# Gathering routed rows in 256-byte pieces, with one block transpose for sixteen, and the router's logits one step earlier

## What is computed

```python
x = x + tanh(g_xattn) * attention(layernorm(x), ctx)      # causal self attention plus cross attention
h = layernorm(x)
out = expert(h, sg, su, sd)                                # shared expert, hidden size 704
probs = softmax(h @ wr.T + rb)                             # 7 routed experts
scores, idx = top_k(probs, 2); scores /= scores.sum()
for e in range(7):
    out += w[..., e] * expert(h, rg[e], ru[e], rd[e])      # w: the two scores, else 0
x = x + tanh(g_ffn) * out
# expert(h, g, u, d) = (silu(h @ g.T) * (h @ u.T)) @ d.T
```

## Time and profile before

| | us |
|---|---|
| median of three runs | 1286.07 |
| lowest and highest run | 1285.67 and 1287.56 |
| time of the profiled execution | 1287.56 |
| its span | 1285.8 |
| PE busy in the span | 1259.2 (98%) |
| DVE, ACT, POOL busy | 1022.2, 851.3, 388.0 |
| granted TensorE clock, mean | 0.994 of full |

### The profile page before, as it was taken

One profiled execution on the slowest core, in us unless ns is written; L12 is line 12 of the kernel. 1 busy time (PEld: TensorE's weight loads), 2 busy tenths in 40 slices (PEclk: granted clock), 3 DMA queues, 4 the chain that ended last, 5 costly groups with the idle time before them and its releaser, 6 DMA issues.

```text
span 1285.8 us, 24163 instructions
## 1 busy us (share of the span) xinstructions
PE 1259.2 (98%) x7868; PEld 689.2 (54%) x7869; DVE 1022.2 (79%) x2357; ACT 851.3 (66%) x1243; POOL 388.0 (30%) x628
## 2 busy tenths in 40 slices
PE   8989999999999999999999999999999999999997
PEld 5645333333333333333333333254568999999996
DVE  6788899999999999999999999554534777777673
ACT  4654788888888888888888888743212555455552
POOL 6565211242242242332422412430001333333332
PEclk9999899999999999999999999999999999999999
DMA  8784332332433523423324334336915122222221
GB/s 250 231 247 144 99 85 85 106 117 79 122 98 85 147 87 99 126 83 107 109 82 129 103 79 141 107 106 166 252 37 148 34 36 35 35 33 37 37 33 21
DMA packets 91864, 133.58 MB, mean 104 GB/s; under 512 B 21387, under 2 KB 56331, under 8 KB 91642
## 3 DMA queue, kind: packets, MB, share of 16 engines
q1 hardware_dynamic: 83162, 122.16, 33.2%
q0 software_dynamic: 7296, 9.97, 4.9%
q10 hardware_dynamic: 1312, 0.27, 0.1%
HBM read 84.36 MB, written 47.55 MB: 103 GB/s over the span
## 4 chain that ended last, share of the span: by engine, by line
PE 90%; DVE 1%; issue 1%; DMA 1%; ACT 1%; POOL 0%; POOLq 0%; SPq 0%; DVEq 0%
PE ps L835 18%; PE ps L989 15%; PE ps L815 14%; PE ps L711 13%; PE ps L1018 8%; PE ps L948 6%; PE ps L963 3%; PE ps L818 3%; PE ps L723 2%; PE ps L789 2%; PE ps L719 2%; PE ps L715 1%; PE ps L923 1%; DMA arena<-rowst 1%; PE ps L803 1%
## 5 line engine op out<-in xcount | busy, mean ns | idle before, releaser
L1510 DVE TENSOR_REDUCE mx<-ps 128x1 f32<-128x512 f32 (+3 forms) x960 | 594.3, 653 | 46.1 <-PE ps L711 19.2
L1180 ACT ACTIVATE arena<-ps 128x1024 f32<-128x1024 f32 (+1 forms) x512 | 480.4, 989 | 67.4 <-PE ps L815 59.8
L835 PE MATMUL ps<-arena 128*32 128x512 f32 (+3 forms) x2048 | 273.0, 567 | 0.8 <-issue 0.4
L1399 POOL TENSOR_SCALAR_AFFINE_SELECT arena<-arena 128x128 f32<-128x128 f32 x256 | 75.3, 294 | 492.2 <-ACT arena L1180 486.0
L815 PE MATMUL ps<-arena 98*128 98x512 bf16 x624 | 198.6, 381 | 1.8 <-DMA arena<-rowst 1.7
L711 PE MATMUL ps<-arena 96*128 96x512 bf16 x576 | 197.6, 382 | 1.9 <-DMA arena<-k_parts 1.4
L989 PEld LDWEIGHTS ps<-work,arena 128*128 128x128 f32 x1672 | 192.7, 192 | 2.9 <-issue 0.9
L989 PE MATMUL ps<-work,arena 128*128 128x128 f32 x1672 | 193.1, 275 | 0.8 <-issue 0.8
L1827 DVE STREAM_TRANSPOSE work<-wp 32x64 f32<-32x64 f32 x608 | 143.3, 236 | 8.5
L835 PEld LDWEIGHTS ps<-arena 128*32 128x32 f32 x2048 | 54.1, 108 | 103.6 <-issue 86.7
L711 PEld LDWEIGHTS ps<-arena 96*128 96x128 bf16 x576 | 53.9, 97 | 96.3 <-DVE mx L1510 55.6
(11 more groups left out here) (191 smaller groups left out, 1527.4 us busy)
## 6 DMA issues: line engine op xcount, KB each, us to landing
o_parts<-work SPq DMA_DIRECT2D x63, 256.0 KB, 2.9
arena<-in_experts SPq DMA_DIRECT2D x56, 176.0 KB
arena<-k_parts SPq DMA_DIRECT2D x48, 198.1 KB, 3.1
arena<-k_parts SPq DMA_DIRECT2D x48, 132.1 KB, 2.9
arena<-in_experts SPq DMA_DIRECT2D x7, 768.0 KB
k_parts<-work SPq DMA_DIRECT2D x16, 300.0 KB, 3.8
q_parts<-work SPq DMA_DIRECT2D x12, 384.0 KB, 3.2
arena<-q_parts SPq DMA_DIRECT2D x48, 96.0 KB, 2.2
```

What stands on the lines that cost most here:

```text
L835: mm = pe.matmul(ps[32 * q:32 * q + VW, 6, first:T], vst[:, r % VR, TT + kt if cross else kt, :], pr[:, c0:c0 + T - first], start=(phase = ...
L1180: act.activation(pr[:, c0:c0 + n], ps[:, 2 * (g % 2):2 * (g % 2) + 2, :].rearrange("p b n -> p (b n)")[:, 0:n], ACT.Exp, scale=SCALE).then ...
L1399: pool.affine_select(out=exps, in_=exps, pattern=[[1, P]], compare_op=ALU.is_ge, fill=0.0, base=0, channel_multiplier=-1).then_inc(S["mask ...
L1510: return dve.tensor_reduce(m, out, AX_X, ALU.max)
```

## The change

Four parts.

1. **Gather in pieces.** `xn_rows` is read as rows of 64 floats (256 bytes), four to a token. `gather(i)` becomes four indirect DMAs, one for each quarter q of `xg`'s columns; lane p of quarter q takes piece p // 32 of the token of lane 32 q + p % 32. With the rows laid out so, `rows_turned` is one DVE transpose of 128x256 in place of sixteen.
2. **Picking.** The row numbers must be laid out to match. POOL builds `pick` (a copy of the identity's blocks) in `wp` and fills `piece_no` with four memsets, behind `logits_turned`. PE's new `pick_lanes()`, four matmuls of 128x128 by 38 columns, stands in the middle of `shared_down(2)`, and DVE's new `piece_rows()` turns them into piece numbers. `rows_ready2` is gone with the cast; `pieces_ready` takes its place before gather(0) and `shared_down(3)`.
3. **Logits earlier.** `logits()` moves ahead of `shared_up(1, 1, 2)`, on PE and ACT, and `turn_logits()` ahead of `shared_up(1, 2, 3)`. DVE's `shared_hidden(1, 1, 2)` and `(1, 2, 3)` each go behind one more piece of the routing.
4. **Banks and DVE's order.** `XN_BANK` no longer uses the bank of the logits, and DVE scales the rows of sequence 2 (`scaled(2)`) two hidden steps earlier.

```diff
-XN_BANK = [0, 1, 4, 5, 6, 7, 4, 5]
+XN_BANK = [0, 1, 4, 5, 6, 4, 5, 6]
...
+        pick = wp[:, :, :].rearrange("p k (q t) -> p (k q) t", q=2)
-        row_at = bv[:, 2, NSLOT:2 * NSLOT].bitcast(U32)
+        piece_row = bv[:, 2, NSLOT:NSLOT + 4 * NSLOT].bitcast(U32).rearrange("p (q i) -> p q i", q=4)
+        piece_no = bv[:, 2, C - 1:C]
+        xn_pieces = xn_rows.rearrange("n (j w) -> (n j) w", w=PIECE)
...
-                    pe.wait_ge(S["rows_ready2"], 1)
+                    pe.wait_ge(S["pieces_ready"], 1)
...
+            def pick_lanes():
+                pe.wait_ge(S["pick_ready"], 5)
+                pe.wait_ge(S["routed"], 1)
+                for q in range(4):
+                    mm = pe.matmul(ps[:, 6, q * NSLOT:(q + 1) * NSLOT], pick[:, q, :], back, start=True, stop=True)
+                mm.then_inc(S["picked"], 1)
...
             turn_xn(3)
+            logits()
             shared_up(1, 1, 2)
-            logits()
-            shared_up(1, 2, 3)
             turn_logits()
-            shared_up(1, 3, IT)
+            shared_up(1, 2, IT)
...
-            shared_down(2)
+            shared_down(2, 0, TT // 2)
+            pick_lanes()
+            shared_down(2, TT // 2, TT)
             shared_down(3)
...
             xn_out(3)
-            shared_silu(1, 1, 2)
             act.wait_ge(S["logits_mm"], 1)
             act.activation(logit_rows, ps7[:, :], ACT.Copy).then_inc(S["logits_out"], 1)
-            shared_silu(1, 2, IT)
+            shared_silu(1, 1, IT)
...
+            pool.wait_ge(S["logits_turned"], 1)
             pool.wait_ge(S["rest_zeros"], 3)
+            pool.tensor_copy(pick.rearrange("p q (j c) -> p q j c", j=4),
+                             ident[:, :].rearrange("p (q c) -> p q c", q=4).unsqueeze(2).to_broadcast([P, 4, 4, QUARTER])
+                             ).then_inc(S["pick_ready"], 1)
+            for j in range(4):
+                pool.wait_ge(S["pick_ready"], j + 1)
+                pool.memset(piece_no[j * QUARTER:(j + 1) * QUARTER, :], float(j)).then_inc(S["pick_ready"], 1)
...
-                pool.indirect_dma_start(out=xg[:, i % 2, :], out_offset=None, in_=xn_rows,
-                                        in_offset=bass.IndirectOffsetOnAxis(row_at[:, i:i + 1], 0)
-                                        ).then_inc(gathered[i % 2], 16)
+                for q in range(4):
+                    pool.indirect_dma_start(out=xg[:, i % 2, q * PIECE:(q + 1) * PIECE], out_offset=None, in_=xn_pieces,
+                                            in_offset=bass.IndirectOffsetOnAxis(piece_row[:, q, i:i + 1], 0)
+                                            ).then_inc(gathered[i % 2], 16)
...
-            shared_hidden(0, 1, 4)
+            shared_hidden(0, 1, 2)
             dve.wait_ge(S["num_in"], 16 * NQ * (NGRP + 2))
             dve.wait_ge(S["den_in"], 16 * NQ * (NGRP + 2))
             scaled(2)
-            shared_hidden(0, 4, 5)
+            shared_hidden(0, 2, 5)
...
+            def piece_rows():
+                dve.wait_ge(S["picked"], 1)
+                dve.tensor_scalar(piece_row.rearrange("p q i -> p (q i)"), ps[:, 6, 0:4 * NSLOT], 4.0, piece_no, ALU.mult, ALU.add
+                                  ).then_inc(S["pieces_ready"], 1)
...
-                for j in range(4):
-                    for r in range(4):
-                        ins = dve.transpose(xgT[j * QUARTER:(j + 1) * QUARTER, b, :, r * QUARTER:(r + 1) * QUARTER],
-                                            xg[r * QUARTER:(r + 1) * QUARTER, b, j * PIECE:(j + 1) * PIECE].rearrange(
-                                                "r (h c) -> r h c", h=2))
+                dve.transpose(xgT[:, b, :, :].rearrange("p h (q r) -> p q h r", q=4),
+                              xg[:, b, :].rearrange("p (q h c) -> p q h c", q=4, h=2)).then_inc(S["xT_ready"], 1)
```

More of the change, by code:

```diff
@@ L355, in program @@
                  "shared_load routed_load route_load up_mm silu_done h_done rest_zeros down_mm acc_done gathered0 gathered1 xT_ready "
-                 "copied up2_mm silu2_done h2_done down2_mm y_ready scattered based routed rows_ready2").split()
+                 "copied up2_mm silu2_done h2_done down2_mm y_ready scattered based routed pick_ready picked pieces_ready").split()
         S = {n: sem(n) for n in names}
@@ L934, in turn_xn @@
                         pe.wait_ge(S["xn_freed"], 1 + XN_BANK.index(XN_BANK[2 * b + k]))
-                    layer_turn(xn_bank(2 * b + k), b, k).then_inc(S["xn_turned"], 1)
+                    layer_turn(ps[:, XN_BANK[2 * b + k], :], b, k).then_inc(S["xn_turned"], 1)
             def shared_up(tb, it0=0, it1=IT):
@@ L1207, in xn_out @@
                     act.wait_ge(S["xn_turned"], n + 1)
-                    act.activation(xnT[:, b, n % 2, :], xn_bank(n), ACT.Copy).then_inc(S["xn_freed"], 1)
+                    act.activation(xnT[:, b, n % 2, :], ps[:, XN_BANK[n], :], ACT.Copy).then_inc(S["xn_freed"], 1)
             def shared_silu(tb, it0=0, it1=IT):
@@ L1460, in _ @@
             pool.wait_ge(S["rows_out"], 32)
-            pool.wait_ge(S["rows_ready2"], 1)
+            pool.wait_ge(S["pieces_ready"], 1)
             gather(0)
@@ L1699, in _ @@
             scaled(3)
-            shared_hidden(1, 0, 2)
+            shared_hidden(1, 0, 1)
             link(dve.memset(lg[:, :, NE:E8], -3e38))
@@ L1719, in _ @@
             first_largest(lg, m1, s1)
-            shared_hidden(1, 2, 3)
+            shared_hidden(1, 1, 2)
             link(dve.scalar_tensor_tensor(out=lg[:, :, :], in0=s1[:, :, :], scalar=-3e38, in1=lg[:, :, :],
@@ L1815, in finish_table @@
                 link(dve.tensor_scalar(back, result_at, float(NTOK), -float(NTOK), ALU.is_ge, ALU.mult))
[L1816 to L1819, removed]
-            def rows_turned(i, b):
-                dve.wait_ge(gathered[b], (i - b) * 8 + 16)
-                for j in range(4):
-                    for r in range(4):
-                        ins = dve.transpose(xgT[j * QUARTER:(j + 1) * QUARTER, b, :, r * QUARTER:(r + 1) * QUARTER],
-                                            xg[r * QUARTER:(r + 1) * QUARTER, b, j * PIECE:(j + 1) * PIECE].rearrange(
-                                                "r (h c) -> r h c", h=2))
-                ins.then_inc(S["xT_ready"], 1)
+                dve.tensor_tensor(back, result_at, back, ALU.add).then_inc(S["routed"], 1)
+            def piece_rows():
+                dve.wait_ge(S["picked"], 1)
+                dve.tensor_scalar(piece_row.rearrange("p q i -> p (q i)"), ps[:, 6, 0:4 * NSLOT], 4.0, piece_no, ALU.mult, ALU.add
+                                  ).then_inc(S["pieces_ready"], 1)
+            def rows_turned(i, b):
+                dve.wait_ge(gathered[b], (i - b) * 32 + 64)
+                dve.transpose(xgT[:, b, :, :].rearrange("p h (q r) -> p q h r", q=4),
+                              xg[:, b, :].rearrange("p (q h c) -> p q h c", q=4, h=2)).then_inc(S["xT_ready"], 1)
             def hidden(i, b):
@@ L1860, in turn @@
                 result(i - 1, 1 - b, first)
-            shared_hidden(1, 3, IT)
+            shared_hidden(1, 2, IT)
             token_weights()
@@ L1875, in _ @@
             finish_table()
+            piece_rows()
             shared_out(2)
```

2 lines of the change are left out of this document (removed).

## The result

The kernel after takes 1328.41 us (median of 4 runs, 1326.69 to 1330.72) where the kernel before took 1285.87 in the same comparison: a ratio of 1.0334, 95% interval 1.0315 to 1.0354. It is 42.5 us slower; the forecast was 2.3, and its range ended at 1291.8. The profiled execution has a span of 1325.2 us, 39.4 more than before, at a mean granted clock of 0.996.

What follows compares the result with a forecast made beforehand. The prediction took PE as the bound, with no idle time in the routed stage. Terms 2.45 - 0.10 + 0.95 - 1.01 = +2.29 us on 1286.07 gave 1288.4 us (+0.18%), range 1285.6 to 1291.8.

Steps and rivals of the forecast that it cites:

- POOL in the loop: Routed loop: four gathers, a scatter and gaps take POOL 7.04 or 7.6 us a turn against PE's 7.50; small excess harmless.
- POOL becomes the bound: Rival, routed loop: gathers costing 1.58 us make POOL's turn 9.4, about 1343 us in all; 0.13 together with serial DMAs.
- if the turn is longer than 7.50: Sign, routed loop: a turn above 7.50 us would show the forecast wrong.
- scaled(2), "nothing": DVE's scaling moved beside POOL's work: 2.38 us, product ready at 867.0 before PE needs it at 867.95, so no cost.
- Logits: logits() straight behind turn_xn(3): PE waits 2.22 us for ACT's copies plus 0.23 restart, +2.45 us.
- bank term: turn_xn(2), second half in bank 4: the following step needs no restart, -0.10 us, between -0.2 and +0.3.
- Pick: Four matmuls of 128x128 by 38 columns on PE's path in shared_down(2): +0.95 us, bounds 0.48 and 1.73.
- Transpose: DVE's one 128x256 transpose replacing sixteen (3.97 us together): taken as 0.5 us, off the chain in the loop.
- The gap before slot 1: Start of routed stage: PE's 0.77 us wait before slot 1 and a 0.24 restart go, -1.01 us.
- The first slots come late: Rival, start of routed stage: slot 0's pieces land late, PE waits up to 3 us, 1289.5 to 1291.5; chance 0.07.
- The wait at the logits isn't there: Rival: ACT or the banks behave otherwise, so without the 2.45 us the time is 1285.9; chance 0.06.
- Faster: Rival, loop: DVE's sixteen transposes slowed PE's reading by 0.15 us a turn; removing them gives 1283.0 us; chance 0.04.

Runs made afterwards that it cites:

- four losing versions: The kernel after with a 32x1 memset behind each slot's second gather, behind its fourth, behind both, or already-met waits between gathers: 1328.74, 1332.46, 1330.43, 1327.51 us.
- Four pieces without scatters: The kernel before with its gather cut into four of 256 bytes a row and the scatter left out for all slots but the last: 1304.11 us.
- the kernel that has nothing else: The kernel before with only the new places of the logits, the bank list and DVE's order: 1288.48 us, ratio 1.0024.
- the kernel after with memsets: The kernel after with a memset of 32x1 on POOL behind each gather: 1289.78 us, ratio 1.0031.
- the two versions without the loss in the loop: The kernel after with a 32x1 memset behind each gather, 1289.78 us, or with a slot's gathers in two pairs, the second behind `h2_done`, 1289.84 us.
- two pieces: The kernel before with its one gather a slot cut into two of 512 bytes a row: 1282.62 us, ratio 0.9982.
- the pairs without scatters: The kernel before with four 256-byte gathers a slot in two pairs, the second behind `h2_done`, and no scatters but the last: 1282.84 us.
- three pieces: The kernel before with its one gather a slot cut into three of 512, 256 and 256 bytes a row: 1282.86 us, ratio 0.9986.

## Why the prediction was wrong

**The step that failed** is "POOL in the loop". Its number was right: a turn of POOL came out at 7.04 to 7.6 us, and the trace has 6.98 from one scatter to the next when POOL doesn't wait (1046.45 to 1053.43). The gather that I took at 0.99 has a median of 952 ns. What failed is the inference from it: that a POOL which keeps up costs nothing. I asked only whether POOL would become the bound, and for the rival "POOL becomes the bound" only what a dearer gather would do. The gather wasn't dearer, POOL had idle time, and the turn still went from 7.50 to 8.6 us. The condition that I wrote, "if the turn is longer than 7.50", came true by another way. The runs show this much of the cause: time is lost with four gathers a turn, with the scatter or without it, and not with three or two; most of it comes without small pieces, and it comes in full without the change's transposes and routing; POOL's busy time alone costs nothing. While POOL issues its groups of DMAs, ACT and DVE take up PE's finished work 3 to 6.5 us late, and they go on 1.2 to 1.35 us after a group of ten has ended. With three gathers ACT is up to 1.6 us late already, and the turn still takes 7.50.

**What stays open** is what holds the others up, and what decides whether it happens. Four memsets of 0.12 us or a step tied to `h2_done` in each turn remove the whole loss; one or two memsets, or waits, remove none; and the same row of twelve gathers was harmful in one kernel and harmless in another. Neither the pace nor the number in a row explains these. A rival is left that no run tests by itself, the pauses. Between 1010 and 1240 the kernel after and its four losing versions go in groups of ten DMAs with no pause over 0.32 us inside, and the versions that lose nothing pause for 0.5 us or more after five DMAs at most. Four pieces without scatters lose with groups of four, though, and whether a pause prevents the lateness or is there because DVE's results come in time, no run tells. No run shows the mechanism, and I name none.

**scaled(2), "nothing"**, was the second miss. I bounded it by the 2.38 us of the earlier trace rows. In the kernel after the four operations stand beside POOL's tensor_tensors at 860.59, 861.82 and 863.27 and take 5.24 us; in other kernels with this order 3.83, 4.08, 4.24 and 4.58. Alone they take 1.38. The prediction left 0.95 us to spare (867.95 less 867.0); 5.24 is 2.86 more than the 2.38 it counted with, and PE waited 1.8:

```profile
PE ps L894 <- ACT xnT L1215: 2.2, 1, 2.2
PE ps L946 <- DVE arena L1651: 1.8, 1, 1.8
PE ps L699 <- ACT xnT L1215: 1.4, 1, 1.4
```

The row taken as a bound was one case of partial overlap, not the worst. The Trainium skill has a rule for it ("SBUF — State Buffer", section "Who interferes with whom"): a tensor_scalar can take a port pair that VectorE shares with GpSimd, and then one of the two waits until the other's instruction is through. The trace agrees with it: three of POOL's operations of about 1.3 us lie in the 5.24, and their 3.85 us and DVE's 1.38 alone make 5.23.

**The terms that held.** Logits: +2.45 was forecast, with a wait of 2.2; the wait is the first row above, and with the bank term of -0.10 (a wait of 1.4 instead of 1.5) the forecast of +2.35 stands against +2.31 in the kernel that has nothing else. Pick: 0.82 us against 0.95. Transpose: 435 ns against 0.5. The gap before slot 1: in the kernel after with memsets the chain has one piece of 9.82 us for slots 0 and 1, twice 4.91, and no gap, so the -1.01 is there once the stops are gone. By these, 2.31 + 0.82 - 1.01 and 2.15 for scaled(2) (the 5.28 us that the stretch grew in the kernel after, less 2.31 and 0.82) make 4.27; the two versions without the loss in the loop are 4.5 us over before. So without the failed step the answer would have been 2 us low.

**The rivals.** "The first slots come late" did not occur as such: no wait of PE for a slot is seen. "The wait at the logits isn't there" was wrong by its row above. "POOL becomes the bound" was priced at 1343 and lies nearer the measured time than the forecast, but not for its reason: a gather took 952 ns and not 1.15 us or more, and POOL had idle time. "Faster": the last kernels show no turn under 7.50, so DVE's sixteen transposes did not slow PE. The rule of the Trainium skill that I cited against the small transfers ("DMA: Bandwidth & Descriptors") speaks of their fixed cost; two and three pieces cost nothing in the loop, and four gathers with a memset behind each cost nothing either, so that cost wasn't the reason, though its advice to join them would have avoided the loss.

## What to carry to other kernels

An engine that keeps up with the loop can still slow it: before a turn is given more indirect DMAs, look at the time between PE's last matmul and the consumer's start in a trace of exactly that version, not only at busy shares. Where such a split is wanted, take the fewest pieces (two and three cost no time here, but three had ACT late already), and time it by itself, because a small edit on POOL's queue moved 38 us one way or the other. A duration read once beside another engine's work is a sample and not a bound; price a move into such work by the sum of the operations that it meets.

## What the hardware showed unexpectedly

ACT and DVE started 3 to 6.5 us after PE's work was done, while idle, and PE stopped for up to 1.0 us at a time, only in kernels with four gathers a turn. In the kernels with one or two gathers a turn, and in three of the four with four gathers that lose nothing, ACT's silu starts 1.82 us into every turn. With three gathers it is up to 3.39 us, and in the fourth, the pairs without scatters, mostly 3.15: late, but not so late that PE has to wait.

The last DRAIN of POOL has different lengths in these kernels, and it lies on the end of the span. In the rows of before, then of two pieces:

```profile
L172 POOLq DRAIN  x1: 8045/8045/8045, 1277.5 to 1277.5; - x1
```

```profile
L172 POOLq DRAIN  x1: 4264/4264/4264, 1275.3 to 1275.3; - x1
```

That is 8.05 us with 76 indirect DMAs in the kernel and 4.26 with 114; three pieces have 6.01 with 152, the kernel after 7.25 with 190. From PE's last matmul to the end of the span before has 9.4 us (1276.43 to 1285.8) and two pieces 6.9 (1272.92 to 1279.8). That 2.5 us is nearly the whole gain of two pieces (2.67), and it is no gain in the loop. Why the length is so isn't shown.
